# A layer norm woven into the edge matrices of the block before it, in a graph network kernel on one Trainium2 core

## What is computed

```
h = jnp.maximum(_layernorm(x, axis=-1), 0.0)
x = x + _L0_gnn_ref(h, edge_index, ...)
...
h = jnp.maximum(_layernorm(x, axis=-1), 0.0)
x = x + _L2_gnn_ref(h, edge_attr_32, src, dst, ...)

# in the third network: a 32x32 matrix for every edge, from the edge's 32 attributes
eh = jax.nn.relu(e_feat @ en1_w.T + en1_b)
w_e = (eh @ en2_w.T + en2_b).reshape(-1, D, D)
for _ in range(STEPS):
    msg = jnp.einsum('ei,eio->eo', out[src], w_e)
```

## Time and profile before

| | |
|---|---|
| median of 3 runs | 8515.5 us (8512.02 to 8523.6) |
| the profiled execution | 8527.12 us |
| its span on the core | 8525.3 us |
| granted TensorE clock, mean over the span | 0.824 of full speed |
| PE busy | 5690.7 us (67%) |
| DVE / POOL / ACT busy | 4696.7 / 3350.0 / 2495.5 us |
| pass P0, from the first transpose to the last pair | 709.8 to 1311.2 us |

### The profile page before, as it was taken

How to read it: one execution, slowest core, us unless ns; L and a number is a source line. 1 busy time by engine, 2 the same in 40 slices (tenths; PEclk the granted TensorE clock), 3 DMA queues, 4 the chain that set the end, 5 groups by cost and what they waited for, 6 DMA issues and landing times.

```text
span 8525.3 us, 71449 instructions
## 1 busy us (share of the span) xinstructions
PE 5690.7 (67%) x21484; PEld 2626.3 (31%) x21492; DVE 4696.7 (55%) x6891; ACT 2495.5 (29%) x4074; POOL 3350.0 (39%) x3658
## 2 busy tenths in 40 slices
PE   2997894431488745576766667675675799999950
PEld 1434442221243311222222222223354444444420
DVE  5563332232444466686867778684375556666640
ACT  1663331110132211111111111112321266666630
POOL 3777745565433333343434353445406200000026
PEclk9997886655799867787878888787797899999975
DMA  2004557896543478797978788796203100000000
GB/s 77 11 9 142 196 207 88 74 78 53 92 91 64 83 237 249 207 264 209 258 214 255 233 231 263 207 266 82 33 1 26 15 10 15 13 15 15 9 18 19
DMA packets 535938, 986.79 MB, mean 116 GB/s; under 512 B 99055, under 2 KB 288259, under 8 KB 535172
## 3 DMA queue, kind: packets, MB, share of 16 engines
q1 hardware_dynamic: 424900, 911.36, 29.8%
q0 software_dynamic: 110656, 70.87, 18.3%
HBM read 778.66 MB, written 203.60 MB: 115 GB/s over the span
## 4 chain that ended last, share of the span: by engine, by line
PE 37%; DMA 18%; POOL 15%; issue 13%; DVE 11%; ACT 5%; SPq 1%; POOLq 0%; DVEq 0%; ACTq 0%
POOL gathered L787 9%; DMA gathered<-table,idx_slot 6%; DMA blocks<-net 5%; PE ps L917 5%; PE ps L1305 4%; DMA ring<-net 4%; PE ps L979 4%; POOL pair_slot L787 2%; PE ps L1067 2%; DVE ring L2093 2%; PE ps L1068 2%; POOL last_of L802 2%; POOL out_dram L901 1%; PE ps L1072 1%; PE ps L1412 1%
## 5 line engine op out<-in xcount | busy, mean ns | idle before, releaser
L787 POOL DMA_INDIRECT gathered<-table,idx_slot x2156 | 2099.4, 974 | 1583.0 <-DVE ring L2093 880.7
L2093 DVE TENSOR_TENSOR ring<-ring,ps 128x1024 f32<-128x1024 f32 (+2 forms) x1008 | 1073.0, 1083 | 499.3 <-DMA ring<-net 464.6
L979 PE MATMUL ps<-ring,mats 128*32 128x512 f32 (+2 forms) x4032 | 709.5, 657 | 372.6 <-DVE ring L2093 311.9
L917 PE MATMUL ps<-mats,gathered 128*128 128x128 f32 x1029 | 217.3, 343 | 1051.1 <-DMA gathered<-table,idx_slot 1001.2
L896 POOL COPY idx_slot<-idx_run_end 128x16 int32<-128x16 int32 (+2 forms) x14 | 2.7, 195 | 1556.3 <-SPq L769 1538.5
L917 PE MATMUL ps<-mats,w 128*128 128x128 f32 x1323 | 279.1, 354 | 449.8 <-DVE w L2556 249.9
L917 PEld LDWEIGHTS ps<-mats,gathered 128*128 128x128 f32 x1029 | 146.5, 171 | 1221.0 <-DMA gathered<-table,idx_slot 1087.9
L780 POOL COPY idx_slot<-idx_row 128x16 int32<-128x16 int32 (+2 forms) x154 | 33.6, 218 | 1085.4 <-SPq L548 1040.5
L2160 DVE SCALAR_TENSOR_TENSOR x_block<-ps,bias,blocks 128x512 f32<-128x512 f32 x300 | 224.7, 749 | 384.3 <-PE ps L1072 384.1
L979 PEld LDWEIGHTS ps<-ring,mats 128*32 128x32 f32 x4032 | 156.0, 125 | 873.4 <-issue 542.4
L2093 DVE TENSOR_TENSOR blocks<-blocks,ps 128x1024 f32<-128x1024 f32 (+2 forms) x336 | 357.4, 1085 | 62.8 <-DMA blocks<-net 58.2
(11 more groups left out here) (279 smaller groups left out, 12241.8 us busy)
## 6 DMA issues: line engine op xcount, KB each, us to landing
ring<-net SPq DMA_DIRECT2D x792, 512.0 KB
blocks<-net SPq DMA_DIRECT2D x264, 512.0 KB
net<-ring SPq DMA_DIRECT2D x176, 512.0 KB, 2.8
table<-w SPq DMA_DIRECT2D x165, 256.0 KB, 2.9
gathered<-table,idx_slot POOLq DMA_INDIRECT x2352, 3.4
ring<-net SPq DMA_DIRECT2D x144, 256.0 KB
x_sp<-x_block SPq DMA_DIRECT2D x79, 256.0 KB, 8.4
x_block<-x_sp SPq DMA_DIRECT2D x79, 256.0 KB, 5.4
```

Of the source, the lines that this page charges most:

```text
L787: pool.indirect_dma_start(dests(k), None, rows, bass.IndirectOffsetOnAxis(ap=dst[:, k:k + 1], axis=0)).then_inc(done, 16)
L917: last = nc.tensor.transpose(dst[:, k * P:k * P + P], src[:, k * P:k * P + P], mat["ident"])
L979: last = mm(message[t * D:t * D + D, 0:wd(i)], adders[2 * m + c], ring[slot][:, c * wd(i):(c + 1) * wd(i)], start=(m == 0 and c == 0), sto ...
L2093: v.tensor_tensor(pair, pair, state, ALU.mult).then_inc(sig["pr"][S_], 1)
```

## The change

The norm of block i+1 is written into the 16 pairs of block i, on all engines; block 0's norm stands ahead of everything. A table says behind which pair each step comes. On PE: the head behind pair 2, centring behind 5, variances behind 7, scales behind 10. On ACT: the copy of x behind its eviction of pair 2, squares and ReLUs behind 5, the roots behind 8. On DVE: eps behind 8, the inverse behind 9, Newton step and spread behind 10, product and scan behind 12. On SP: the x stores behind the store of pair 4, the attribute load behind that of pair 10. The norm gets the bank pD of each side for itself (head, centred values, variances and scales share it one after the other), and the hidden activations go to the tiles w[3] and not w[0], which the norm's squares use. The waits on the scan, on the norm and on the evictions at a block's border go. Nothing of POOL's stream is changed, and the instructions of the other engines are the same ones in another order. The diff, without the hunk that cuts ACT's `layer_norm` (L1590 to L1597) into `moments` (Square and ReLU) and `deviations` (the root):

```diff
@@ -397,6 +397,10 @@
             for b in wide_space[par]:
                 b.x, b.small, b.spread = x_pair[par][b.u], pC[b.u], pC[b.u]
         lower, upper = slice(0, 2 * D), slice(2 * D, 4 * D)
+        first_space = [Space(u) for u in SPACES]
+        for b in first_space:
+            b.centred = b.small = b.spread = pD[b.u]
+        attr_hidden = [w[3][k][:] for k in (0, 1)]
         message, both_z = pD[S_], pC[S_]
         copied4 = (pA[D_], pB[D_], pC[D_], pD[D_])
         adders = [mats[:, MATS.index("sums0") + c // T, c % T * D:c % T * D + D] for c in range(CHUNKS)]
...
@@ -694,14 +698,21 @@
 
             q, q2 = p_["P0"], p_["WE"]
 
-            def body(i, par, j, q=q, q2=q2):
+            def attributes(i):
                 for u in (0, 1):
                     spent(sp, "ehp", u, q2.n("ehp", u, i, 0))
                 sp.dma_start(attr_in[:, :, 0:wd(i)], ins["edge_attr_T"].rearrange("d (t e) -> d t e", t=T)[:, :, col(i)]
                              ).then_inc(dma["ld_ea"][0], 16)
+
+            def x_store(i):
                 for u in SPACES:
-                    ready(sp, "xb", u, q.n("xb", u, i))
+                    sp.wait_ge(sig["xb"][u], q.n("xb", u, i) + 1 + CREDIT)
+                    settle(sp)
                     sp.dma_start(x_sp[u, :, col(i)], fit(xb[u], i)).then_inc(dma["st_x"][u], 16)
+
+            attributes(0)
+            x_store(0)
+            for i in range(EB):
                 for k in range(PAIRS):
                     n = i * PAIRS + k
                     for b in (0, 1):
...
@@ -709,7 +720,10 @@
                         settle(sp)
                     sp.dma_start(net[n:n + 1, :, 0:2 * wd(i)].rearrange("a p f -> p (a f)"), ring[n % RING][:, 0:2 * wd(i)]
                                  ).then_inc(dma["st_we"][n % RING], 16)
-            sweep(sp, EB, body)
+                    if i + 1 < EB and k == 4:
+                        x_store(i + 1)
+                    if i + 1 < EB and k == 10:
+                        attributes(i + 1)
             for u in SPACES:
                 stored(sp, "st_x", u, q.last("st_x", u) + 1)
             for k in range(RING):
...
@@ -1278,33 +1292,46 @@
 
             for par in (0, 1):
                 ready(pe, "ends_d", par, q.last("ends_d", par))
-            q = p_["P0"]
-
-            def body(i, par, j, q=q, q2=p_["WE"]):
+            q, q2 = p_["P0"], p_["WE"]
+
+            def first_head(i):
                 for u in SPACES:
-                    spent(pe, "weo", u, q2.n("weo", u, i))
-                for u in SPACES:
-                    pe.wait_ge(dma["ld_g0"][2 * u + par], gathered_by(j + 1, par))
-                    spent(pe, end_of["P0"][u], u, q.n(end_of["P0"][u], u, i))
-                    turn(fit(pA[u], i), G[par][u], q_of(i)).then_inc(sig["head"][u], 1)
-                layer_norm(q, space, i)
-                ready(pe, "scan", S_, q.n("scan", S_, i))
-                ready(pe, "ln", D_, q.n("ln", D_, i))
-                landed(pe, "ld_ea", 0, q2.n("ld_ea", 0, i))
-
-                def hidden(t):
-                    mm(fit(pA[t % 2], i), en1[:], attr_in[:, t, 0:wd(i)], start=True, stop=True).then_inc(sig["ehp"][t % 2], 1)
-                hidden(0)
+                    pe.wait_ge(dma["ld_g0"][2 * u + i % 2], gathered_by(i // 2 + 1, i % 2))
+                    pe.wait_ge(sig["ln"][u], q.n("ln", u, i) + CREDIT)
+                    turn(fit(pD[u], i), G[i % 2][u], q_of(i)).then_inc(sig["head"][u], 1)
+
+            def first_norm(i, stage):
+                for b in first_space:
+                    if stage is variances:
+                        pe.wait_ge(sig["ln_relu"][b.u], q.n("ln_relu", b.u, i) + 1 + CREDIT)
+                    stage(q, b, i)
+
+            def attr_in_hidden(i, t):
+                mm(fit(pA[t % 2], i), en1[:], attr_in[:, t, 0:wd(i)], start=True, stop=True).then_inc(sig["ehp"][t % 2], 1)
+
+            def matrix_pair(i, t, k):
+                for c in (k % T * 2, k % T * 2 + 1):
+                    b = c % 2
+                    pe.wait_ge(sig["weo"][b], q2.n("weo", b, i, k) - 1 + CREDIT)
+                    mm(fit((pB, pC)[k % 2][b], i), en2[:, c * P:c * P + P], fit(attr_hidden[t % 2], i), start=True, stop=True
+                       ).then_inc(sig["wep"][b], 1)
+
+            first_head(0)
+            for stage in (centre, variances, scales):
+                first_norm(0, stage)
+            for i in range(EB):
+                ahead_of = {2: lambda: first_head(i + 1), 5: lambda: first_norm(i + 1, centre),
+                            7: lambda: first_norm(i + 1, variances), 10: lambda: first_norm(i + 1, scales)} if i + 1 < EB else {}
+                pe.wait_ge(dma["ld_ea"][0], 16 * (i + 1))
+                attr_in_hidden(i, 0)
                 for t in range(T):
                     if t + 1 < T:
-                        hidden(t + 1)
-                    ready(pe, "eh", t % 2, q2.n("eh", t % 2, i, t // 2))
-                    for c in range(CHUNKS):
-                        b, k = c % 2, t * (CHUNKS // 2) + c // 2
-                        pe.wait_ge(sig["weo"][b], q2.n("weo", b, i, k) - 1 + CREDIT)
-                        mm(fit((pB, pC)[k % 2][b], i), en2[:, c * P:c * P + P], fit(w[0][t % 2], i), start=True, stop=True
-                           ).then_inc(sig["wep"][b], 1)
-            sweep(pe, EB, body)
+                        attr_in_hidden(i, t + 1)
+                    pe.wait_ge(sig["eh"][t % 2], q2.n("eh", t % 2, i, t // 2) + 1 + CREDIT)
+                    for k in range(t * (CHUNKS // 2), (t + 1) * (CHUNKS // 2)):
+                        matrix_pair(i, t, k)
+                        if k in ahead_of:
+                            ahead_of[k]()
             tables("T0", "P0")
 
 
...
@@ -1791,27 +1824,36 @@
             for par in (0, 1):
                 stored(act, "st_d", par, p_["ENDS"].last("st_d", par) + 1)
 
-            def body(i, par, j, q=q, q2=p_["WE"]):
+            q2 = p_["WE"]
+
+            def first_copy(i):
                 for u in SPACES:
                     ready(act, "head", u, q.n("head", u, i))
                     stored(act, "st_x", u, q.n("st_x", u, i))
-                    f(fit(xb[u], i), fit(pA[u], i), ACT.Copy).then_inc(sig["xb"][u], 1)
-                layer_norm(q, space, i)
-
-                def hidden(t):
-                    ready(act, "ehp", t % 2, q2.n("ehp", t % 2, i, t // 2))
-                    f(fit(w[0][t % 2], i), fit(pA[t % 2], i), ACT.Relu, bias=one_col("en1_b")).then_inc(sig["eh"][t % 2], 1)
-                hidden(0)
+                    f(fit(xb[u], i), fit(pD[u], i), ACT.Copy).then_inc(sig["xb"][u], 1)
+
+            def attr_relu(i, t):
+                act.wait_ge(sig["ehp"][t % 2], q2.n("ehp", t % 2, i, t // 2) + 1 + CREDIT)
+                f(fit(attr_hidden[t % 2], i), fit(pA[t % 2], i), ACT.Relu, bias=one_col("en1_b")).then_inc(sig["eh"][t % 2], 1)
+
+            first_copy(0)
+            moments(q, first_space, 0)
+            deviations(q, first_space, 0)
+            for i in range(EB):
+                ahead_of = {2: lambda: first_copy(i + 1), 5: lambda: moments(q, first_space, i + 1),
+                            8: lambda: deviations(q, first_space, i + 1)} if i + 1 < EB else {}
+                attr_relu(i, 0)
                 for t in range(T):
                     if t + 1 < T:
-                        hidden(t + 1)
+                        attr_relu(i, t + 1)
                     for k in range(t * (CHUNKS // 2), (t + 1) * (CHUNKS // 2)):
                         n, c = i * PAIRS + k, k % (CHUNKS // 2) * 2
                         act.wait_ge(sig["wep"][0], q2.n("wep", 0, i, k) + 1 + CREDIT)
                         stored(act, "st_we", n % RING, n // RING)
                         f(ring[n % RING][:, 0:wd(i)], fit((pB, pC)[k % 2][0], i), ACT.Identity, bias=en2b[:, c:c + 1]
                           ).then_inc(sig["weo"][0], 1)
-            sweep(act, EB, body)
+                        if k in ahead_of:
+                            ahead_of[k]()
             tables("T0")
 
 
...
@@ -2346,19 +2388,28 @@
 
             q = p_["P0"]
 
-            def body(i, par, j, q=q, q2=p_["WE"]):
-                layer_norm(q, space, i, [blk(h[u], i) for u in SPACES])
+            q2 = p_["WE"]
+
+            def first_apply(i):
+                norm_apply(q, first_space, i, [blk(h[u], i) for u in SPACES])
                 ready(dve, "ln", S_, q.n("ln", S_, i))
                 run_sums(q, i, blk(h[S_], i))
 
-                for t in range(T):
-                    for k in range(t * (CHUNKS // 2), (t + 1) * (CHUNKS // 2)):
-                        n, c = i * PAIRS + k, k % (CHUNKS // 2) * 2 + 1
-                        dve.wait_ge(sig["wep"][1], q2.n("wep", 1, i, k) + 1 + CREDIT)
-                        stored(dve, "st_we", n % RING, n // RING)
-                        v.tensor_scalar(ring[n % RING][:, wd(i):2 * wd(i)], fit((pB, pC)[k % 2][1], i), en2b[:, c:c + 1], None, ALU.add
```

(17 more changed lines are left out.)

6 lines of the change are left out of this document (5 added, 1 removed).

## The result

| | before | changed |
|---|---|---|
| median (6 runs each, same chip) | 8520.28 us (8512.02 to 8545.81) | 8477.94 us (8467.5 to 8484.13) |
| the profiled execution | 8527.12 us | 8484.13 us |
| its span | 8525.3 us | 8482.3 us |
| granted TensorE clock, mean over the span | 0.824 | 0.827 |
| last pair of P0 ends | 1311.2 us | 1268.1 us |

The ratio is 0.9946, with a 95% interval of 0.9932 to 0.996: 0.5% faster, some 46 us by the ratio (the two medians lie 42 us apart). In the profiled executions the stage ends 43 us earlier and the span is 43 us shorter, so all of the gain lies in the pass that was changed. The forecast was 8465 us within 8450 to 8500, by POOL's gathers becoming the bound.

A forecast was written before the change was run, and what follows sets the result against it. PE was taken to bound P0 at 47.82 us a block; woven, it needs 40.2, so POOL's gathers at 41.83 set the pace. Last gather at 1173.2 plus PE's remaining work ends at 1260.9: 50 us less, 8465 us, range 8450 to 8500.

The forecast's parts named there:

- The bound: Pass P0, full blocks: POOL's gathers at 41.83 us a block set the pace over PE's woven block of 40.2 us.
- The sum: P0's end: last pair at 1260.9 us instead of 1311.2, so 50 us less and a median of 8465 us.
- The last gather's landing: Block 12's last gather in P0: issued by 1171.4 us, landing 3.0 us from its issue, at 1173.2.
- the tail: PE's work in P0 after block 12's last gather lands: rest of block 11, then blocks 12 and 13, 1173.2 to 1260.9 us.
- The pace's upper bound: POOL's gathers in P0: DVE's spread copies and products could hold them up, adding 2.2 us, for 44.0 us a block.
- rival B: P0's gathers slow down to 44.0 us a block: ten blocks, 22 us later, 8487 us; chance 0.07.
- PE's terms: PE's full block in P0: pairs 28.05, hidden matmuls 4.2, norm steps; 38.1 us together, 40.2 with the wait at the scales.
- The wait at the scales: PE's scales behind pair 10 wait for DVE's eviction, refinement and spread: 2.1 us a block, the one wait not covered.
- The granted clock 1.00 from block 6 on: A sign of the forecast: PE in P0 is granted the full 2.4 GHz clock from block 6 onwards.
- Rival A: PE's clock falls at its stops in P0: 4 us a fall, one a block gives 44.2 us, 8495 us; chance 0.17.
- Rivals C and D: P0: C, four 2 us stops, 46 us a block, 8513 us, chance 0.08; D, three clock falls, 52.3, 8584, chance 0.06.
- those covered steps: ACT's and DVE's norm steps lying under PE's pairs in P0: waits costed at 0, or 2 us a block if cover fails.

## Why the prediction was right

**The bound.** POOL's gathers set the pace, as forecast: heads wait for gathers, POOL waits for nobody, and the edit that shortens POOL's part and leaves all the work in place took 17.5 us more off the pass. An edit that relieved PE alone left the pace at 42.27. Not every head waited, though: seven of the nine steady ones did.

**The sum.** Forecast was the last pair at 1260.9; it ended at 1268.1. The 7.2 us are the sum of four small ones. The pass started 1.2 us later in this execution. The pace was 42.28 against 41.83, 4.5 over ten blocks. Of these, 3.5 are the three gaps of 1.47 us in place of 0.30, and 1.0 is gathers held longer by the scan and the spread copies. The gaps could have been read before the change: the forecast took its pace from the copies at 753.06 and 878.54, a stretch that has none of them, while over the seven blocks up to the copy at 1048.20, before POOL waits for PE, the same timeline gives 295.14 / 7 = 42.16. The last gather's landing took 2.5 us after the copy that follows it, against 1.8. And the tail was 88.5 against 87.7, though two falls of the clock lie in it (1180 to 1184 and 1197 to 1201, 3.4 us of work lost) that the sum did not have: its other terms were too large by nearly as much. That the tail came out within 1 us is in part luck. Of the expected 50 us, 43 came in the profiled execution and some 46 by the ratio.

**The pace's upper bound** of 44.0 (rival B) had a real mechanism, but at a small part of its size. The scan was in the 41.83 already. Of what B added, the spread copies do hold gathers that begin beside them, as at 1158.22 above, but only four times in ten blocks and for 0.5 us in all; beside products and evictions gathers stay at 0.94 to 0.97. The Trainium skill, "SBUF — State Buffer", section "SBUF: two separate sides", says that some VectorE instructions hold a port that GpSimd needs; the trace shows gathers held by the scan and, for less long, by the spread copies.

**PE's terms.** Work without waits was put at 38.1 and measured 37.5. The wait at the scales was put at 2.1 and is 1.8 to 1.9. The block was put at 40.2 and measures 40.95 where gathers don't bind, since a term was missing: 1.6 us for one fall of the clock. The terms that were too large hid half of that. "The granted clock 1.00 from block 6 on" was wrong, it is 0.97 from that block's head to the end.

**Rival A** is that missing term. It had the fall at 4 us, in which case PE would have been the bound at 44.2. A fall of 3 to 4 us at 1.2 GHz costs 1.6, the difference of 40.95 and 37.5 less the wait, and that still fits beside the gathers' 42.28. Its margin was thin, 1.3 us a block, so it is in part luck that the missing term did not decide the pace. The Trainium skill, "TensorE: Matmul & The Clock Gate", section "HAM oscillation — how this bites in real kernels", has waits in a loop of matmuls bringing the low clock back; the waits of its example are longer than the 1.8 us at the scales here, so the forecast applied it further than it goes. The windows agree that it comes back, and the run with the scales a pair later that it goes with the wait; but it comes about once a block, now behind the wait and now behind the variances, not at every stop.

**Rivals C and D** asked for stops at every step, or for two falls a block of 4 us. Head, centring and variances show no wait of ACT's or DVE's steps, and there is one fall. The cost of 0 for those covered steps held.

What stays open: what holds ACT and DVE on the two other chips; whether the change helps there, where the five runs of woven kernels came out between 0.5% faster and 0.4% slower than the kernel before; what part of the 46 us the banks and tiles bring alone; and what the gaps of 1.47 us on POOL are. That a slower gather would have left the kernel before untouched rests on POOL's wait for PE in the earlier trace rows; the run meant to show it could not.

## What to carry to other kernels

When work is woven under another loop, price the next clock in line first: here PE's block went from 47.8 to 41 us, but gathers asked for 42.3, and the cheapest further gain was on POOL, in two tiny copies. Relieve the bound and its runner-up together: half the gathers alone gave 10 us of P0, a step moved by one pair beside it 38 more, 31 of them in the steady blocks. Leave a pair between the one whose eviction stands ahead of DVE's step and PE's step that needs its result. And take a pace from as long a stretch as the trace has: three blocks missed what seven show.

## What the runs showed of the hardware

A single wait of 1.8 us a block cost 3.4. With it, and half the gathers left out, the granted clock fell to 0.50 once in 41 us; without it, it stayed at 1.00 over nine blocks, though the 16 short matmuls of the variances (1.84 us) were still there.

A gather that begins inside DVE's scan of 1.28 us ends 0.75 or 0.76 us after the scan: in the changed kernel's pass it takes 1.12 to 1.78 us in place of 0.94. One that begins beside the spread copies takes 1.00 to 1.15 there; one beside an eviction or a product does not take longer.

An index copy of 0.2 us takes 1.0 with the hand-over to the first gather (0.81 idle before it), 0.73 more than going straight on, and six in a row took 1.50.

The same kernel took 8517 us on one chip and 9144 and 9202 on two others, with waits there of up to 59.5 us on DVE and 59.1 on ACT that the profile puts down to no engine of the core.
